# All weights loaded during the first attention, one fence between stages, in a kernel of eight chained stages

## The reference

```
x = x + window_attention(ln(x))   # 16 heads of 8, window 64
x = x + mixture(ln(x))            # 8 experts, top 2, and a shared gated part
x = x + causal_attention(ln(x))   # one head of 128
x = x + mixture(ln(x))            # the same weights again
x = x + cope_attention(ln(x))     # attention over the batch axis of 2
x = x + local_stack(ln(x))        # 6 layers: local attention (16 heads of 64, window 32,
                                  # rotary), token shift, layer norm, gated feed-forward
x = x + linear_attention(ln(x))   # its four weights are built from small factors
x = x + local_stack(ln(x))        # the same 6 layers and weights again
```

## Time and profile before

| what | value |
|---|---|
| three executions | 4439.8, 4441.26, 4445.46 us (median 4441.26) |
| the profiled execution's own time | 4439.44 us |
| its span, first to last instruction | 4438.1 us |
| PE busy | 3859.1 us (87%) |
| DVE busy | 3062.1 us (69%) |
| ACT busy | 2568.4 us (58%) |
| POOL busy | 2649.1 us (60%) |
| mean granted TensorE clock | 0.915 of 2.4 GHz |
| transfers on SyncE's queue | 270.33 MB, 23.9% of 16 DMA engines' time |

### The profile page before, as it was taken

The page is one execution under the profiler, slowest core; times in us unless marked ns, Lnnn a source line. Parts: engine busy times, 40 slices in busy tenths (PEclk is TensorE's granted clock), DMA queues, the critical chain, the costliest instruction groups (busy, mean ns, idle before and its releaser), DMA issues. The chain is left out here.

```text
span 4438.1 us, 158857 instructions
## 1 busy us (share of the span) xinstructions
PE 3859.1 (87%) x66864; PEld 2706.7 (61%) x66864; DVE 3062.1 (69%) x6301; ACT 2568.4 (58%) x4921; POOL 2649.1 (60%) x2218
## 2 busy tenths in 40 slices
PE   7968694399999999999999623999999999999996
PEld 5645453266667666676676422676666676766764
DVE  4446464678777777777777347777777777777773
ACT  3325251266666676666676401666667676666664
POOL 2029074477667676676776203776766767767662
PEclk7569797699999999999999855999999999999998
DMA  0010100133332333333322101333323333233222
GB/s 15 1 33 1 35 1 5 45 93 78 83 85 70 90 80 82 81 82 78 83 65 71 45 7 35 93 82 81 91 65 90 80 85 85 73 87 83 64 71 55
DMA packets 307779, 280.48 MB, mean 63 GB/s; under 512 B 158840, under 2 KB 205696, under 8 KB 307072
## 3 DMA queue, kind: packets, MB, share of 16 engines
q1 hardware_dynamic: 307072, 270.33, 23.9%
HBM read 55.22 MB, written 1.05 MB: 13 GB/s over the span
## 5 line engine op out<-in xcount | busy, mean ns | idle before, releaser
L1459 ACT ACTIVATE m_sq<-PS 128x512 f32<-128x512 f32 x384 | 226.2, 595 | 197.6 <-PE PS L1312 160.8
L1459 ACT ACTIVATE l_sq<-PS 128x512 f32<-128x512 f32 x384 | 226.2, 595 | 196.5 <-PE PS L1312 160.1
L1724 POOL TENSOR_TENSOR l_Pm<-l_Pm,l_rs 128x1024 f32<-128x1024 f32 x96 | 182.9, 1905 | 238.2 <-DVE l_rs L1596 238.2
L1724 POOL TENSOR_TENSOR m_Pm<-m_Pm,m_rs 128x1024 f32<-128x1024 f32 x96 | 182.9, 1905 | 233.7 <-DVE m_rs L1596 233.7
L124 POOL TENSOR_TENSOR rstd<-rstd,minus_half 128x4 f32<-128x4 f32 x40 | 41.9, 1046 | 378.5 <-DVE rstd L120 378.5
L1614 DVE TENSOR_TENSOR XN<-PS,XN 128x128 f32<-128x128 f32 x192 | 56.2, 293 | 279.4 <-PE PS L1364 279.3
L1583 DVE TENSOR_TENSOR l_QR<-PS,l_rot 128x512 f32<-128x512 f32 x192 | 131.8, 687 | 163.2 <-ACT l_sq L1459 163.2
L1583 DVE TENSOR_TENSOR m_QR<-PS,m_rot 128x512 f32<-128x512 f32 x192 | 131.8, 686 | 163.0 <-ACT m_sq L1459 163.0
L1719 POOL TENSOR_TENSOR m_QR<-m_QR,m_UQ 128x1024 f32<-128x1024 f32 x96 | 227.7, 2372 | 24.0 <-DVE m_UQ L1586 24.0
L1719 POOL TENSOR_TENSOR l_QR<-l_QR,l_UQ 128x1024 f32<-128x1024 f32 x96 | 227.7, 2372 | 23.3 <-DVE l_UQ L1586 23.3
L1719 POOL TENSOR_TENSOR l_KR<-l_KR,l_UK 128x1024 f32<-128x1024 f32 x96 | 227.0, 2364 | 0.2 <-DVE l_UK L1586 0.2
(11 more groups left out here) (388 smaller groups left out, 11840.8 us busy)
## 6 DMA issues: line engine op xcount, KB each, us to landing
l_V<-l_Vt SPq DMA_DIRECT2D x576, 128.0 KB
m_V<-m_Vt SPq DMA_DIRECT2D x576, 128.0 KB
l_V<-l_Vt SPq DMA_DIRECT2D x384, 64.0 KB
m_V<-m_Vt SPq DMA_DIRECT2D x384, 64.0 KB
l_wqkv<-l_wqkv_dram SPq DMA_DIRECT2D x72, 128.0 KB, 2.4
m_wqkv<-l_wqkv_dram SPq DMA_DIRECT2D x72, 128.0 KB, 2.5
l_rot<-l_rot_dram SPq DMA_DIRECT2D x24, 256.0 KB, 3.8
m_rot<-l_rot_dram SPq DMA_DIRECT2D x24, 256.0 KB, 3.8
```

Source lines behind the costliest of these rows:

```text
L1459: ac.activation(sq[:, c, b * 512:(b + 1) * 512], PS[:, 2 * c + b, :], ACT.Square).then_inc(sq_out)
L1724: gp.tensor_tensor(pm, pm, over(rs[:, :], 2, [P, 16, 2 * LW]), ALU.mult).then_inc(pn_out)
```

## The change

The weights of all later stages get buffers of their own, for the whole program or (for the mixtures, the causal attention and the attention over the batch) until the first stack begins. The second mixture uses the first one's copy. `load_early` issues 71 transfers for them and the 33 of the stack's layer 0 behind the first fence, so beside the window attention, and SyncE waits for the 71 before the fence that closes that stage. The seven `load` calls of the later stages and their second fences are gone.

The two stacks share one set of weight buffers. The semaphores of these loads are no longer cleared by fences: their counts run on through the second stack (`base`). In its last layer the first stack loads layer 0 again, for the second. The memsets of a stack move behind its fence: three short ones ahead of the square roots, six behind them; only the parts that are read before they are written are cleared. A semaphore `ready` holds TensorE until the first three are done, and VectorE and SyncE until all are.

```diff
+        early_in, w_attn, w_rot, w_ffn = (ctx.enter_context(nc.semaphore(n)) for n in ("early_in", "l_w_attn", "l_w_rot", "l_w_ffn"))
+        wqkv = sb("l_wqkv", P, 2, 3 * INNER)
...
+        d_bias, d_gain = sb("d_bias", P, 4, D), sb("d_gain", P, 4, D)
+        first = ctx.enter_context(ExitStack())
...
+        f_w13, f_w2 = se("f_w13", P, 2, E_N, D), se("f_w2", P, E_N, D)
...
+        def load_early():
...
+            for to, src in pairs:
+                sp.dma_start(to, src).then_inc(early_in, 16)
+            load_rotary(0)
+            for k in range(14):
+                load_attention(0, k)
+            load_ffn(0)
+            sp.wait_ge(early_in, 16 * len(pairs))
...
                 fence()
+                load_early()
...
-                load((wqk[:, :], t["b_wqk"]), (wov[:, :], t["b_wov"]), (future[:, :], t["b_future"]))
-                fence()
...
+                base = 0 if tag == "l_" else DEPTH
...
-                load((mask[:, :, :], t["l_mask"]), (ident_b[:, :], t["ident_b"]))
-                for part in (XST[64:, :], xsh[0:1, :, :, :], kT[:, :, 0:LW], Vt[:, :, :]):
-                    G.step(gp.memset(part, 0.0))
-                    G.wait()
-                for part, value in ((hT[64:, 2, :], 1.0), (sums2[:, :, :], 1e-24), (zero[:, :], 0.0), (eps[:, :], EPS)):
-                    G.step(gp.memset(part, value))
-                    G.wait()
-                fence()
...
-                            te.wait_ge(w_attn, 224 * (layer(n) + 1))
+                            te.wait_ge(w_attn, 224 * (base + layer(n) + 1))
...
+                    te.wait_ge(ready, 1)
                     for g in range(NG):
                         te.wait_ge(xn_out, g + 1)
...
+                    ve.wait_ge(ready, 2)
                     for s in range(-2, 4 * FG + 8):
...
-                        gp.wait_ge(w_rot, 96 * (l + 1))
+                        gp.wait_ge(w_rot, 96 * (base + l + 1))
...
+                    for column in (0, L):
+                        G.step(gp.memset(XST[64:, column:column + 1], 0.0))
+                        G.wait()
+                    gp.memset(kT[:, :, 0:LW], 0.0).then_inc(ready)
                     for g in range(NG):
                         norm_root(g)
+                    gp.wait_ge(rstd_out, NG)
+                    for part, value in ((Vt[P - LW:, 1, :], 0.0), (xsh[0:1, :, :, :], 0.0), (hT[64:, 2, :], 1.0), (sums2[:, :, :], 1e-24),
+                                        (zero[:, :], 0.0)):
+                        G.step(gp.memset(part, value))
+                        G.wait()
+                    gp.memset(eps[:, :], EPS).then_inc(ready)
                     rotary(0)
...
-                    load_rotary(0)
-                    for k in range(14):
-                        load_attention(0, k)
-                    load_ffn(0)
+                    sp.wait_ge(ready, 2)
...
-                        if 0 <= s and l < DEPTH:
+                        if 0 <= s and (l < DEPTH or l == DEPTH and base == 0):
```

More of the change, by code:

```diff
@@ L106, in group, with load_attention, load_rotary @@
             return src[:, 4 * g:4 * g + 4, :]
+        def load_attention(l, k):
+            if k < 12:
+                part = slice(k * 256, (k + 1) * 256)
+                sp.dma_start(wqkv[:, l % 2, part], t["l_wqkv"][l % DEPTH][:, part]).then_inc(w_attn, 16)
+            else:
+                half = slice((k - 12) * 4, (k - 11) * 4)
+                sp.dma_start(wo[:, l % 2, half, :], t["l_wo"][l % DEPTH].rearrange("(c p) d -> p c d", p=P)[:, half, :]).then_inc(w_attn, 16)
+        def load_rotary(l):
+            par, m = l % 2, l % DEPTH
+            for r in range(4):
+                sp.dma_start(rot[:, par, r, :, :], t["l_rot"][r].rearrange("(i p) d -> p i d", p=P)).then_inc(w_rot, 16)
+            sp.dma_start(qs[:, par, :], t["l_qs"][m:m + 1, :].to_broadcast([P, LD])).then_inc(w_rot, 16)
+            sp.dma_start(ks[:, par, :], t["l_ks"][m:m + 1, :].to_broadcast([P, LD])).then_inc(w_rot, 16)
@@ L875, in cope_attention @@
                 att = sl("att", P, NT, D)
-                load(*[(w[:, n * D:(n + 1) * D], t[("c_wq", "c_wk", "c_wv")[n]]) for n in range(3)],
-                     *[(bqkv[:, n * D:(n + 1) * D], row(("c_bq", "c_bk", "c_bv")[n], D)) for n in range(3)],
-                     (wo[:, :], t["c_wo"]), (bo[:, :], row("c_bo", D)),
-                     *[(pos_rows[:, d, :], t["c_pos"][0, d:d + 1, 0:3].to_broadcast([P, 3])) for d in range(DH)])
-                fence()
                 def part(s, n):
@@ L1017, in linear_attention @@
                 ws = {n: sl("w" + n, P, D) for n in "qkvo"}
[L1018 to L1021 removed]
+                bs = {n: d_bias[:, m4, :] for m4, n in enumerate("qkvo")}
+                fact, blocks = d_fact, d_blocks
+                g1, b1, g2, b2 = (d_gain[:, k, :] for k in range(4))
                 tmp = sl("tmp", P, D)
@@ L1855, in build @@
         cope_attention()
+        first.close()
         local_stack("l_")
```

132 lines of the change are left out of this document (59 added, 73 removed).

## The result

The changed kernel takes 4363.22 us (median of four executions, 4355.26 to 4370.58) against 4441.93 us for the kernel before in the same set; the ratio is 0.9823, with a 95% interval from 0.9806 to 0.9839. Two later sets of the same kernel gave 4354.23 us (ratio 0.9806, 0.9788 to 0.9825) and 4353.91 us (0.9807, 0.9784 to 0.9831). The forecast was 4358 us, with a range from 4348 to 4368 us, so it holds in all three sets. The comparisons leave out one execution of a later experiment, `late_d`, which took 5144.74 us at a mean granted clock of 0.699.

The account below looks back on a forecast made before the run. The prediction saw eight stages in a chain without overlap, with 90.3 us in seven gaps of fence, loads, fence. 82.6 + 1.7 - 2.0 = 82.3 us off gave 4357.1, hence a 4358 us median; own range 4348 to 4368 us.

Parts of the forecast that it names:

- The gaps: Seven gaps between stages, 90.3 us, keep one fence of 1.1 us each, 7.7 us in all; 82.6 us leave.
- the upper bound of 2.1 us: Most a bare gap might take: the smallest gap with loads, 5.0 us, less its loads' 2.9 us.
- the gaps were not loads: Rival: engines need the old gaps to be supplied after a fence; each keeps about 3 us more, 4379 us; 4%.
- The early loads: 104 transfers beside the window attention cost 0 on the path, up to 3 us for disturbed instruction supply.
- The start of a stack: First rotation about 17.2 us after first statistics, 18.1 before, ended by GpSimd's tables; 0.85 us gained per stack.
- The term's other end: At a stack's start, memsets and VectorE hold each other up: 3.8 us on GpSimd's chain, each stack 2.9 us later.
- Layer 5: First stack's last layer, now loading the second stack's layer 0, costs 2.0 us more; bounds 0 and 3.9.
- The sum: Whole kernel: 82.6 + 1.7 - 2.0 = 82.3 us saved, median 4358 us, 1.9% faster.
- Transfers inside the stacks: Rival: a shift of starts makes the second stack as slow as the first, 4370 us; 8% for the slow side.
- The clock upwards: Rival: in the window attention TensorE's clock stays up after 63 us, saving 68 us, 4290 us; 7%.
- Downwards: Rival: in the window attention TensorE's clock is lost at 43 us; 20 us turn into 40, 4378 us; 3%.
- A mixture loses its clock: Rival: one of two mixtures stays at 1.2 GHz throughout, 134 us more, 4492 us; 2%.

Follow-up runs that it names:

- late_d: Changed kernel with the linear attention's 40 loads back in front of it, with wait and second fence; three executions 4370.91 to 4390.11 us, ratio 0.9864.
- no_layer_loads: Changed kernel without weight loads for layers 2 to 5 of the first stack and all of the second; two early-loaded sets reused; 4332.09 us, ratio 0.9759.
- after_third: The changed kernel, unchanged, measured a third time; 4353.91 us (4348.39 to 4363.64).

## Why the prediction was right

**The gaps** (82.6 us forecast). 90.31 - 7.46 = 82.85 us. A bare fence was put at 1.1 and is 1.03 to 1.10; the upper bound of 2.1 us is what two fences cost. The rival "the gaps were not loads" is refuted by the changed kernel's own gaps, which keep no 3 us, and by `late_d`, where the gap comes back with the loads.

**The early loads** (0, up to 3). SyncE is done at 69.9 us, before the 80 that were named. The window attention took 241.15, 240.50 and, with 40 transfers fewer, 240.93 us (`late_d`), with 33 more, 240.21 us (`no_layer_loads`), against 240.3 before. So the loads cost at most 0.9 us there. The 254.37 us of `after_third` are the clock's, and are taken up under the rivals.

**The start of a stack** (17.2 us, 0.85 earlier each). Measured 17.29 and 0.8 earlier. The six clearings took from 787.74 to 790.86, 3.1 us for the 3.05 forecast, the products 5.2. The term's other end was contention, taken as 0. Here are VectorE's normalising instructions of the last group (ns: shortest, median, longest), four before the memsets and four beside them:

```profile
L221 DVE TENSOR_SCALAR XN<-X,meanvar,rstd x4: 342/344/347, 786.5 to 787.2; 128x128 f32<-128x128 f32 x4
```

```profile
L221 DVE TENSOR_SCALAR XN<-X,meanvar,rstd x4: 859/954/1054, 787.7 to 789.0; 128x128 f32<-128x128 f32 x4
```

The same shows in the second stack (858 to 1053 ns, for memsets at 2644.36 and 2645.37 us). There is contention with a memset, and VectorE pays all of it: 344 becomes 954 ns, while the memsets of 1024 elements take 0.95 and 0.98 us beside it, against 0.94 without it. Neighbours overlap in time, so these durations must not be added up: the four took 2.2 us together (787.7 to 789.9), where four alone take 1.1. The prediction's 4 x 0.95 us for the other end had that fault. The 0 was right for GpSimd's chain, which is the one that counts, though the reason given (the row is of another operation) was not. The Trainium skill's rule ("SBUF — State Buffer", Who interferes with whom) that the two take turns on a shared port pair agrees with VectorE's side; the 0.5 us that the prediction worked out from it for GpSimd's side did not come.

**Layer 5** (+2.0, bounds 0 and 3.9). The output adds of the first stack in the changed kernel, fourteen tiles of layer 4 and of layer 5, each from the last add of the layer before on; they answer to the earlier trace rows:

```profile
L1647 DVE TENSOR_TENSOR XN<-PS,XN x15: 290/291/294, 1917.7 to 2152.9; 128x128 f32<-128x128 f32 x15
...
L1647 DVE TENSOR_TENSOR XN<-PS,XN x15: 290/292/294, 2189.9 to 2424.3; 128x128 f32<-128x128 f32 x15
```

Layer 4 took 235.2 us (238.9 before, with nothing changed in it) and layer 5, now with the loads, 234.4 (235.0 before, without them). By these rows the loads would be free. But a single layer moves by as much as the whole difference that I divided: the same tiles of layer 4 of the second stack took 236.9, 235.1 and 240.1 us in three traces of the changed kernel. The mean of many does better. Layers 1 to 4 of both stacks take 237.0 us in the five traces with loads (40 values, 235.1 to 241.8) and 235.0 us in `no_layer_loads` (8 values, 233.7 to 236.0), so the loads cost 2.0 us a layer. And in `no_layer_loads`, where no layer has loads, layer 5 still takes only 232.4 and 232.5 us: the other 2.5 us of the old difference belong to the rotary products, or to whatever else the last layer lacks. So the value was right, but halving 3.9 us was a guess that happened to fall near it.

**The sum.** 82.3 us forecast; 84.1 us measured in the span. 82.85 are the gaps, 1.45 the stage stretches, less 0.2 at the ends; the starts' 1.6 us and layer 5's 2 us lie inside a scatter of the stacks from 1704.2 to 1712.1 us in the traces of the changed kernel and its two variants with the same stacks, so these two terms are confirmed by their own rows and not by the sum. The medians of the second and third set, 4354 us, lie 4 us under the forecast; that of the first, 4363 us, lies 5 us over it.

**The rivals.** *Transfers inside the stacks*: the scatter is real (1704.2 to 1712.1 us), and no stack reached the old 1715 us. It was gone in the one trace without weight loads (1697.12 and 1696.94 us); one trace doesn't show that it goes with them. *The clock upwards*: it stayed at 0.50 from 63 to 252 us, at 99% busy, with transfers beside it or not. *Downwards*: this one happened, in one traced execution, for 14 us where 20 were forecast. It doesn't set the median of the second and third set; in the first set three of four executions look like it, so there it probably does, and accounts for that set's higher median. I had put the loss at 43 us; the rows show a fall that comes before 46 us in both of these traces, and what differs is the return. The kernel before shows long executions of the same kind, so the change doesn't create it; its share in 4 of 13 against 3 of 29 executions leaves open whether the change makes it more frequent. *A mixture loses its clock*: no; the mixtures' stretches show a granted clock of 0.87 to 0.89 in every trace.

## What to carry to other kernels

Between stages that are separated by fences, a gap can be taken apart in its rows into fence, issue and landing; transfers put beside a long stage that doesn't use the queue give back all but the fence. Judge a queue by what stands behind it: 1.4 us more of issuing in front of each group's V transfers put 61 / 48 = 1.3 us on the time for each of the 48 groups, while 104 transfers before 70 us, with nothing behind them, cost nothing. And before a difference of two layers is used as a price, look how much one layer moves between executions (here 5 us of 237).

## What the hardware did that I had not expected

- A 127-partition transfer keeps the DMA share at 0.07 to 0.08 for over 6 us, and the next issue on that queue takes 6.5 us (48 of 48, for a transfer of one partition, in three pieces of 64 elements or in one). Behind a transfer of the same size on 128 partitions it takes 0.78 us. At a stack's end VectorE is idle for 10.2 us, in each stack.
- Beside a memset on GpSimd, a VectorE instruction of 344 ns takes up to 1054 ns, four of them 2.2 us instead of 1.1, and the memset no longer than alone (0.95 to 0.98 against 0.94 us).
- TensorE's clock, fallen to 1.2 GHz before 46 us, was back at 2.4 GHz from 46 to 63 us in one execution and not in another of the same kernel, with TensorE busy 9.4 of 10 us before it in both. It cost 14 us, the largest difference of a stage between the traces of this kernel.
